# Three attention layers and a dense tower on one core: one stationary for both heads' Y per row half, inputs copied to the other partition half, a score product per head

## What is computed

```python
def _mhsa(x, Wq, Wk, Wv, Wr):          # 3 layers, 2 heads, dh = 32
    q, k, v = (x @ Wq), (x @ Wk), (x @ Wv)         # each reshaped to (B, 39, 2, 32)
    scores = jnp.einsum('bihd,bjhd->bhij', q, k)
    attn = jax.nn.softmax(scores, axis=-1)
    out = jnp.einsum('bhij,bjhd->bihd', attn, v).reshape(B, n, D)
    return jax.nn.relu(out + x @ Wr)
...
embed_x = emb_table[X + offsets[None, :]]
att = embed_x
for i in range(3):
    att = _mhsa(att, WQ[i], WK[i], WV[i], WR[i])
att_output = relu(att.reshape(B, 2496) @ Wlin)
h = relu(embed_x.reshape(B, 2496) @ W1 + b1)       # 512
h = relu(h @ W2 + b2)                              # 256
return sigmoid(att_output + relu(h @ W3 + b3))
```

## Time and profile before

| | us |
|---|---|
| median of the runs (3) | 2034.81 |
| profiled execution, span | 2034.7 |
| PE busy | 1914.9 (94%) |
| DVE busy | 1690.5 (83%) |
| ACT busy | 1351.5 (66%) |
| POOL busy | 893.3 (44%) |

### The profile page before, as it was taken

How to read it: one execution, slowest core, us unless ns; L and a number is a source line. 1 busy time by engine, 2 the same in 40 slices (tenths; PEclk the granted TensorE clock), 3 DMA queues, 4 the chain that set the end, 5 groups by cost and what they waited for, 6 DMA issues and landing times.

```text
span 2034.7 us, 105018 instructions
## 1 busy us (share of the span) xinstructions
PE 1914.9 (94%) x44960; PEld 1692.9 (83%) x44960; DVE 1690.5 (83%) x3771; ACT 1351.5 (66%) x3609; POOL 893.3 (44%) x949
## 2 busy tenths in 40 slices
PE   1499999999999999999999999999999999999998
PEld 0387888888888888888888888888888888888887
DVE  3477889889898888979888898888889898888987
ACT  1366666667666676766766776666776667676665
POOL 6544354444535454354544435354453545444000
PEclk9899999999999999999999999999999999999998
DMA  4210111111111111111111111111111111110000
GB/s 113 60 31 25 31 27 32 29 30 31 28 33 28 31 30 29 32 28 32 29 30 30 29 33 27 32 28 30 31 28 34 28 32 29 30 31 26 20 20 16
DMA packets 67859, 64.71 MB, mean 32 GB/s; under 512 B 24056, under 2 KB 54792, under 8 KB 67400
## 3 DMA queue, kind: packets, MB, share of 16 engines
q1 hardware_dynamic: 47432, 37.52, 6.3%
q0 software_dynamic: 19968, 20.49, 5.3%
HBM read 27.24 MB, written 0.01 MB: 13 GB/s over the span
## 4 chain that ended last, share of the span: by engine, by line
PE 86%; DVE 5%; issue 4%; ACT 3%; another core or an unknown queue 1%; POOL 1%; SPq 0%; DMA 0%; ACTq 0%
PE SV L479 20%; PE Ob L496 14%; PE X L464 12%; PE X L457 8%; PE X L459 5%; PE X L458 5%; PE Mb L432 3%; PE Mb L433 3%; PE Mb L434 3%; PE Ob L457 3%; PE Ob L458 2%; PE Ob L459 2%; PE Ob L423 2%; PE Mb L450 1%
## 5 line engine op out<-in xcount | busy, mean ns | idle before, releaser
L355 POOL DMA_INDIRECT emb<-L_rec_emb_table,idx_t x624 | 646.9, 1037 | 752.4 <-PE Ob L496 551.2
L742 DVE TENSOR_REDUCE den<-sd 103x16 f32<-103x624 f32 x384 | 308.0, 802 | 225.6 <-ACT sd L616 211.0
L479 PE MATMUL SV<-yv,xs 64*39 64x142 f32 x12288 | 456.0, 285 | 21.2 <-ACT v_sb L618 13.4
L479 PEld LDWEIGHTS SV<-yv,xs 64*39 64x39 f32 x12288 | 349.8, 113 | 68.0 <-issue 39.6
L600 ACT ACTIVATE xs<-Ob 128x312 f32<-128x312 f32 x256 | 110.4, 431 | 383.6 <-PE Ob L496 383.6
L722 DVE TENSOR_REDUCE mx<-SV 103x8 f32<-103x312 f32 x768 | 332.7, 473 | 37.0 <-PE SV L479 28.7
L496 PEld LDWEIGHTS Ob<-pt,v_sb 39*32 39x32 f32 x12288 | 272.1, 106 | 96.5 <-issue 96.0
L464 PE MATMUL X<-ident,pn 103*103 103x103 f32 x3072 | 343.0, 255 | 0.0
L496 PE MATMUL Ob<-pt,v_sb 39*32 39x39 f32 x12288 | 326.4, 198 | 8.9 <-issue 8.5
L332 POOL COPY xs<-embT 64x256 f32<-64x256 f32 x300 | 239.1, 797 | 211.6 <-ACT embT L560 80.7
L727 DVE TENSOR_TENSOR sd<-SV,mx 103x312 f32<-103x312 f32 x768 | 330.2, 470 | 0.1
(11 more groups left out here) (81 smaller groups left out, 2749.2 us busy)
## 6 DMA issues: line engine op xcount, KB each, us to landing
v_x<-v_sb SPq DMA_DIRECT2D x768, 39.0 KB
emb<-L_rec_emb_table,idx_t POOLq DMA_INDIRECT x624
xs<-L_rec_W SPq DMA_DIRECT2D x19, 256.0 KB
w<-L_rec_W SPq DMA_DIRECT2D x1, 512.0 KB
idx_in<-r_X SPq DMA_DIRECT2D x1, 312.0 KB, 3.8
b_b<-L_rec_b SPq DMA_DIRECT2D x1, 256.0 KB
b_b<-L_rec_b SPq DMA_DIRECT2D x1, 128.0 KB
w_b<-L_rec_W SPq DMA_DIRECT2D x1, 128.0 KB
```

Of the source, the lines that this page charges most:

```text
L355: nc.gpsimd.indirect_dma_start(out=emb[:, n % ER, f % 2 * D:(f % 2 + 1) * D], out_offset=None, in_=table, in_offset=bass.IndirectOffsetOnA ...
L479: last = nc.tensor.matmul(SV[64 * b:64 * b + F, at:at + YR], x_pair(u, e, p), yv[64 * e:64 * e + D, l, p, :], start=True, stop=True, skip_ ...
L742: nc.vector.tensor_reduce(den[:], pe_sb[:], AX.X, ALU.add).then_inc(den_ready, 1)
```

## The change

1. **Y.** The stationary becomes 64x128: A_0 beside A_1 for one row half. For each half e three matmuls (64 rows, 128 columns, moving 64x312) give both heads' Y of the sample half e: head h on partitions 64 h of bank X_e. Six matmuls as before, alternating between the row halves.
2. **Scores.** Head h's Y now lies on partitions 64 h for both sample halves, so x of the other half is needed there: SyncE copies each unit's x to the other partition half (`xx`, 4 buffers, two DMAs per unit of 64 partitions x 1248 bytes), once x is there and the scores of unit s-4 are done. A score product is made per head: 64 matmuls per step instead of 32, stationary 64x39, moving 64x71 (39 columns of Y, 32 value columns). The value columns are of the head `odd ^ h`, so that each head's values come out on the partitions where `attended` wants them.
3. **`v_x` is gone**, its two DMAs per unit and the wait `v_moved`; `scores` waits for `x_moved` instead.
4. Before Y of step s PE waits once for both `pt` copies of unit s-3, where each product waited for its own.
5. The SV regions are 128 columns wide instead of 256, and the PSUM patterns of the DVE and ACT instructions that read SV change with them, not their sizes.
6. **Start.** The weight tensors have 256 columns per layer instead of 384; A_h is stored by 2 copies instead of 4; the value columns of `yv` are filled by 12 copies of 64 x 256 elements after the weight split, instead of 3 of 128 x 512 before it.

```diff
             for u in range(TOTAL):
-                sp.wait_ge(v_ready, u + 1)
-                for b in range(2):
-                    lo, hi = 64 * b, 64 * (1 - b)
-                    sp.dma_start(v_x[hi:hi + F, u % VS, :, :], v_sb[lo:lo + F, u % VS, 1 - b, :, :]).then_inc(v_moved[u % VS], 16)
+                if u % NU < UL:
+                    sp.wait_ge(shuffled, (u // NU + 1) * NB * 4)
+                else:
+                    sp.wait_ge(x_new, outputs(u - UL))
+                at_least(sp, sv_ps, 2 * (u - XXS + 1))
+                for e in range(2):
+                    lo, hi = 64 * e, 64 * (1 - e)
+                    sp.dma_start(xx[hi:hi + D, u % XXS, :],
+                                 xs[lo:lo + D, x_buffer(layer_of(u)), layer_cols(u)]).then_inc(x_moved[u % XXS], 16)
...
+            def scored(l, slot):
+                for w, x, first, final in ((w_hi, x_lo, True, False), (w_lo, x_hi, False, False), (w_hi, x_hi, False, True)):
+                    for e in range(2):
+                        lo = 64 * e
+                        last = nc.tensor.matmul(XB[e][:, 0:C], w[lo:lo + D, l, 0:128], x[lo:lo + D, slot, :],
+                                                start=first, stop=final)
+                        if final:
+                            last.then_inc(y_ps, 1)
...
                 for j in range(2):
                     if j == 0:
                         at_least(pe, v_ready, u)
-                    for pp in range(2):
-                        for e, b in ((0, 0), (1, 1), (0, 1), (1, 0)):
-                            p = 4 * j + 2 * pp + b
-                            at = ((2 * j + e) * 2 + pp) * SR
-                            last = nc.tensor.matmul(SV[64 * b:64 * b + F, at:at + YR], x_pair(u, e, p),
-                                                    yv[64 * e:64 * e + D, l, p, :],
-                                                    start=True, stop=True, skip_group_check=True)
+                        pe.wait_ge(x_moved[u % XXS], 32 * (u // XXS + 1))
+                    for e in range(2):
+                        for pp in range(2):
+                            for h, odd in ((0, 0), (1, 0), (0, 1), (1, 1)):
+                                p = 4 * j + 2 * pp + odd
+                                b = odd ^ h
+                                at = (2 * j + h) * W + (2 * e + pp) * SR
+                                last = nc.tensor.matmul(SV[64 * b:64 * b + F, at:at + YR], x_half(u, e, p, h),
+                                                        yv[64 * h:64 * h + D, l, e * UP + p, :],
+                                                        start=True, stop=True, skip_group_check=True)
                     last.then_inc(sv_ps, 1)
...
             def attended(u):
-                pe.wait_ge(v_moved[u % VS], 32 * (u // VS + 1))
...
-                    for h in range(H):
-                        at_least(pe, pt_ready, 2 * (u - 1) + h + 1)
-                        product(XB[h][:, 0:C], layer_of(s), h * 128, s % XS).then_inc(y_ps, 1)
+                    at_least(pe, pt_ready, 2 * u)
+                    scored(layer_of(s), s % XS)
```

More of the change, by code:

```diff
@@ L43, in autoint @@
     G = UP
-    SR = 256
-    YR = HF + D
+    SR = 128
+    YR = F + DH
     VS = 3
@@ L48, in autoint @@
     XS = 5
+    XXS = 4
     EXP_AT, PV_AT, NEW_AT = 1, 2, 3
@@ L144, in autoint @@
         x_lo = sb("x_lo", [128, XS, C], F32R)
[L145 to L148, removed]
+        w_all = embT[:, 1].rearrange("q c b -> q (c b)")[:, 0:L * (2 * 128 + D)].rearrange("q (l c) -> q l c", l=L)
+        yv = sb("yv", [128, L, 2 * UP, YR])
+        v_sb = sb("v_sb", [KR, VS, 2, H, G // 2, DH])
+        xx = sb("xx", [128, XXS, C])
         mx = sb("mx", [KR, G, H])
@@ L213, in autoint @@
         v_ready = sem("v_ready")
-        v_moved = [sem(f"v_moved{k}") for k in range(VS)]
+        x_moved = [sem(f"x_moved{k}") for k in range(XXS)]
         mx_ready = sem("mx_ready")
@@ L282, in layer_cols, with x_half @@
             return slice((u % UL) * C, (u % UL + 1) * C)
-        def x_pair(u, e, p):
+        def x_half(u, e, p, h):
+            if h != e:
+                return xx[64 * h:64 * h + D, u % XXS, p * F:(p + 1) * F]
             at = (u % UL) * C + p * F
@@ L454, in dense, with residual @@
                     first_layer(t + 1, 0)
[L456 to L459, removed]
+            def residual(l, slot):
+                nc.tensor.matmul(Ob[:, 0:C], w_hi[:, l, 128:256], x_lo[:, slot, :], start=True, stop=False)
+                nc.tensor.matmul(Ob[:, 0:C], w_lo[:, l, 128:256], x_hi[:, slot, :], start=False, stop=False)
+                nc.tensor.matmul(Ob[:, 0:C], w_hi[:, l, 128:256], x_hi[:, slot, :], start=False, stop=True)
+            def scored(l, slot):
[6 more added lines that the diff above has]
+                            last.then_inc(y_ps, 1)
             def transposes(u, j):
@@ L491, in attended @@
                     for e in range(2):
-                        g = (2 * j + e) * 2 + pp
+                        i = 2 * e + pp
                         for h in range(H):
                             lo, po = 64 * h, 64 * e + DH * h
-                            v = v_sb[lo:lo + F, u % VS, h, g, :] if b == h else v_x[lo:lo + F, u % VS, g, :]
-                            last = nc.tensor.matmul(Ob[po:po + DH, p * F:(p + 1) * F], v, pt[lo:lo + F, g, b, :],
+                            last = nc.tensor.matmul(Ob[po:po + DH, p * F:(p + 1) * F],
+                                                    v_sb[lo:lo + F, u % VS, j, odd ^ h, i, :],
+                                                    pt[lo:lo + F, 4 * j + i, odd ^ h, :],
                                                     start=False, stop=True, skip_group_check=True)
@@ L522, in _ @@
                         pe.wait_ge(embT_ready, chunk_count(*chunk_at(s - 1)))
-                    product(Ob[:, 0:C], layer_of(u), 256, u % XS)
+                    residual(layer_of(u), u % XS)
                 if chunk_at(s):
@@ L607, in _ @@
                     at_least(act, sv_ps, 2 * s)
-                    for h in range(H):
-                        act.wait_ge(y_ps, 2 * s + h + 1)
-                        nc.scalar.copy(yv[:, layer_of(s), :, h * F:(h + 1) * F],
-                                       XB[h][:, 0:C].rearrange("q (p f) -> q p f", f=F)).then_inc(y_ready, 1)
+                    for e in range(2):
+                        act.wait_ge(y_ps, 2 * s + e + 1)
+                        nc.scalar.copy(yv[:, layer_of(s), e * UP:(e + 1) * UP, 0:F],
+                                       XB[e][:, 0:C].rearrange("q (p f) -> q p f", f=F)).then_inc(y_ready, 1)
                 u = s - EXP_AT
@@ L617, in _ @@
                     at_least(act, o_ps, u - VS + 1)
-                    nc.scalar.copy(v_sb[:, u % VS, :, :, :], sv_values).then_inc(v_ready, 1)
+                    nc.scalar.copy(v_sb[:, u % VS].rearrange("q j h i c -> q (j h i) c"), sv_values).then_inc(v_ready, 1)
                 if s < TOTAL and ts == H1T_AT:
```

40 lines of the change are left out of this document (20 added, 20 removed).

## The result

| | before | after |
|---|---|---|
| median of the runs (4 each, one chip) | 2035.41 us | 2284.92 us |
| lowest and highest | 2032.1, 2038.5 | 2278.53, 2295.32 |

The ratio is 1.122, with an interval of 1.119 to 1.125. The forecast was 2020 us with a range up to 2058. It was wrong in its sign and in its range.

What follows compares the result with a forecast made beforehand. Two nearly equal loops bound the kernel, PE's own work and one through ACT. 2034.7 - 28 (slack) + 8 (scores) + 6 (supply) - 1 (start) = 2020 us; its own range 1996 to 2042, the stated range up to 2058.

Steps and rivals of the forecast that it cites:

- the instruction supply: Unexplained PE gaps inside `attended`, 21.3 us, would grow in proportion to PE's instructions: +6 us, bounds -5 and +36.
- Sign (4): Check on PE's unexplained gaps in `attended` and the scores' line: no more than 30% above those of before.
- Rival C: Scores and `attended` as one dense stretch can't be fed: scores +0.1 us per step, gaps +15 us, 2059 us; chance 19%.
- Y: Y's matmul pairs on PE run side by side, saving PE 0.33 us per step (0 to 0.43).
- (1): Check on Y: six matmuls from first start to the tower's first in 0.6 to 0.7 us.
- rival B: Y's pairs don't overlap and PE pays a 0.1 us tiling switch: 2074 us; chance 6%.
- Scores by themselves: 64 score matmuls instead of 32 on PE, same columns streamed: +0.02 us per step, +8 us in all (0 to +38).
- Rival E: Each score matmul costs what it does now, 35 ns, whatever its columns: about 2430 us; chance 2%.
- The slack: Only the ACT loop's slack before the scores is gained, 0.18 us in 128 steps plus 5 us elsewhere: -28 us.
- (6): Check on step lengths: with relu 4.96 to 5.0 us as now, without 4.7 to 4.75 instead of 4.9.
- Rival A: PE's own work bounds all steps, so each wins 0.31 us: about 1920 us; chance 5%.
- The x copies: SyncE's DMAs of x to the other partition half have three steps, 15 us, and delay nothing: cost 0.

Runs made afterwards that it cites:

- e1: The kernel after without the copies of x to the other partition half and without the wait for them; 2280.08 us, ratio 1.121.
- e2: The kernel before with each score matmul of 142 columns split into two of 71, nothing else changed; 2327.11 us, ratio 1.146.
- e4: The kernel before with only the change's Y, six matmuls in pairs on the two row halves; 2021.16 us, ratio 0.9925.
- e5: The kernel before with only the second half (j = 1) of the score matmuls split, 48 per step; 2191.45 us, ratio 1.081.
- e12: The kernel before with paired Y and 32 extra small matmuls per step between Y and the tower, repeated on another chip; 2244.39 us, ratio 1.102.
- e14: The kernel before with the value copy on DVE at positions 8 to 17 only, repeated on another chip; 2024.98 us, ratio 0.995.
- e13: The kernel after with the scores in two halves, four transposes ahead of each; 2377.91 us, ratio 1.167.
- e6: The kernel after with half of the matmuls of `attended` left out; 2021.14 us, ratio 0.9957.
- e8: The kernel before with paired Y and 32 extra small matmuls per step between Y and the tower; 2188.23 us, ratio 1.100.
- e9: The kernel before with paired Y and 64 extra small matmuls per step between Y and the tower; 2414.63 us, ratio 1.215.
- e10: The kernel before with the value copy on DVE at positions 8 to 17 only, first run; 1967.63 us, ratio 0.9896.

## Why the prediction was wrong

**The step that failed is the instruction supply**, put at +6 us with bounds of -5 and +36. It came to 154.9 + 37.9 = 193 us of idle PE by the waits alone, beside 21.3 before, and what the clock took after the gaps comes on top. Sign (4), gaps no more than 30% above those of before, failed. I had read two things wrongly. First, I scaled the 21.3 us of the earlier trace rows "in proportion" to PE's instructions, by 27%, as if the new gaps were more of the same. They are of another kind. Before, 2 of the 22 us of idle time in `attended` stand at a packet's edge and half of it at position 9, like the two gaps of the earlier trace rows, which aren't at an edge either; after, 151 of 155 us stand at the edge. So the row said nothing about the term. Second, I looked at `attended`'s own 128 instructions in 0.6 us, a stretch shorter than a packet. What counts is how fast whole packets are used up. From one packet's edge to the next PE took at least 4.8 us before, and 1.7 us after, in e1 and in e2. And 152 of the gaps ended 2.2 to 2.9 us from their packet's start.

**Rival C had the mechanism and not the size.** It named the one stretch of scores and `attended` and its 256 instructions, and gave 2059 us, by gaps of 15 us and scores longer by 0.1 us. Its argument against itself, that `attended` takes instructions almost twice as fast, is true of the rate and beside the point, since `attended` alone is half a packet. That the clock would fall with the gaps, to 0.955 over the span, stood nowhere.

**Y: right in kind, too large.** The timeline of PE after, beside the earlier trace rows:

```profile
1001.79 0.41 PE L474 MATMUL X<-x_lo,w_hi 64*128 64x312 f32 x2
1002.04 0.30 PE L474 MATMUL X<-x_hi,w_lo 64*128 64x312 f32 x2
1002.18 0.30 PE L474 MATMUL X<-x_hi,w_hi 64*128 64x312 f32 x2
1002.41 0.50 PE L440 MATMUL Mb<-w_hi,c_lo 128*128 128x512 f32 x1
1003.75 0.89 PE L482 MATMUL X<-ident,pn 103*103 103x103 f32 x8
```

The pairs start together. From the first to the tower it is 0.62 us instead of 0.97, within the 0.6 to 0.7 that (1) asked for, and rival B is out. But the tower's second matmul starts 0.34 us after its first (at 1002.75), where it was 0.23 before, so of the 0.35 us PE keeps some 0.24: by the medians the transposes start 1.97 us after Y where it was 2.20. The forecast had 0.33.

**Scores by themselves: right.** Where the chain has them whole, 64 take 1.13 to 1.20 us (1.20 in the row 1103.57), against 1.11 to 1.18 for 32; +0.02 us was the term. Rival E, a price per matmul, is out. By the Trainium skill's figure in rival E (TensorE: Matmul & The Clock Gate, Wait — 56ns, not 53.3ns?), the loss would by estimate have been some 190 us, all in the scores. That this is of the size of the measured 250 us is chance, for the scores without a gap hardly grew, and over 60% of the loss stands between `attended` and Y.

**The slack: right in kind, too large.** e4 gained 12.7 us where the forecast had 28, from four positions instead of eight. In e4 the typical step with relu stayed at 4.96, as (6) said, and those that gained came to 4.65 to 4.79. Rival A, PE as the bound everywhere, is out: ACT's list sets the scores of many steps. In after it still does so in over half of them; this is its value copy in one, to be read against the earlier trace rows:

```profile
1096.43 0.61 ACT L638 COPY v_sb<-SV 103x512 f32<-103x512 f32 x1
```

The value copy ended at 1097.04 and the scores followed at 1097.14, 0.93 us after the first transpose (at 1096.21) where 0.82 is enough in steps that ACT doesn't hold up.

**The x copies: right.** e1 shows no cost, and (5), no wait for `xx`, held. **The start** can hardly be judged. The first scores start 2.6 us earlier (72.3 instead of 74.9), the 21st 4 us later, and waits in between come and go: before's profiled execution has one wait of 12.3 us for `v_sb` at its second scores, after's has none there, e5, e12 and e14 have one again.

With the supply as it was before, the measured slack and scores and the forecast's -1 for the start would give about 2034.7 - 12 + 9 - 1 = 2031 us. That is worked out, not run. The bounds of the forecast's sum, all taken at their ends, add up to 1991 to 2050; its range of 1996 to 2042 is narrower than that.

**What stays open.** (a) What sets the start of a fetch. A plain rule, "256 instructions in less than a fetch takes", does not fit: e5 has stalls at blocks of 4.5 to 5 us, e12 has 101 blocks under 4 us and no edge gaps. What does fit is this. A packet as a rule starts only after PE has passed the edge before it, 1.2 us later in the median of after, up to 4.5, and PE stalls if it gets to the next edge less than 2.3 us after that start. In after this was so for 161 of the 432 blocks from the 21st on, and 154 of these stalled, of the others 12; in e5 it was 116 with 93 stalls, of the others 4; in e12 it was 3. In e5's stalled blocks the packet had started 3.2 us (median) after the edge, in e12's 101 fast ones 0.5 us. Why the start comes so late in some blocks is open. (b) The gaps that don't stand at the edge: 57 us of those over 0.3 us in after, most of before's, at position 9 above all, the 0.4 us of e13 and the rest in e6. (c) Why the chip where before takes 1989 us shows almost none of the gaps under (b), and what after would take there; it wasn't run. (d) The share of the clock: gaps and low clock come together in every run here, though not in proportion (e13 has 182 us at the edges and a clock of 0.979), and no run separates them.

## What to carry to other kernels

Count PE's instructions in the densest 5 us, loads included and a fp32 matmul as two pairs, and compare it with the length of that stretch; a change that keeps the columns and doubles the instructions isn't free, and it may be paid for in the stretch behind it. Before scaling idle time that nothing explains, find where it stands (here: its place in every 256 instructions, and its position in the tile): a small amount of one kind says nothing about another that the change can bring, and such a term has no upper end in proportion. Where two loops are nearly equal, only the slack of the other one is to be had, and it has to be counted position by position.

## What the hardware showed that I had not expected

PE's instructions came in packets of 256 (+96 packets for +24,576, from e8 to e9), each started as a rule only after PE had passed the edge before it, and an empty supply stopped PE for up to 2.3 us with nothing else to wait for. The longest stops came at one fixed place in each 256, and mostly in `attended`, at the end of the dense stretch. After the one shown the granted clock was 0.66 for 4.5 us. And the same program differed between chips by 2.3% (1989.23 against 2035.87 us); by the traces of e10 and e14 the difference stands at the start and in gaps at one position of the tiles, not at packet edges.
